# A pre-norm block with linear attention on one core: phase 1 without the V projection, wo scaled by rows

## The reference

```
y  = ln(x)
a  = ln(y) * ln1_g + ln1_b
q, k, v = a @ wq, a @ wk, a @ wv                     # 16 heads of 16
phi(t) = elu(t) + 1 = min(exp(t), 1) + relu(t)
kv = sum over tokens of phi(k)^T v,  z = sum of phi(k)   # per sequence and head
r  = y + ((phi(q) kv) / (phi(q) z + 1e-6)) @ wo
h  = ln(r) * ln2_g + ln2_b
s  = r + gelu(0.1 * clip(round(h @ w1 / 0.1))) @ w2       # w1 256x1024, w2 1024x256
x1 = x + s
out = x1 + (ln(x1) @ CB^T) * SCB / 127 + bias
```

## Time and profile before

| | |
|---|---|
| median of 3 runs | 613.63 us |
| profiled execution | 617.22 us, span 615.5 us |
| TensorE busy | 582.9 us (95%) |
| VectorE busy | 469.2 us (76%) |
| ScalarE busy | 411.4 us (67%) |
| GpSimd busy | 382.2 us (62%) |
| fp32 and fp32r products at L929, turns at L947 | 66% and 8% of the chain that ended last |
| HBM read, written | 20.45 MB, 8.39 MB |

### The profile page before, as it was taken

The page is one execution under the profiler, slowest core; times in us unless marked ns, Lnnn a source line. Parts: engine busy times, 40 slices in busy tenths (PEclk is TensorE's granted clock), DMA queues, the critical chain, the costliest instruction groups (busy, mean ns, idle before and its releaser), DMA issues.

```text
span 615.5 us, 12217 instructions
## 1 busy us (share of the span) xinstructions
PE 582.9 (95%) x3838; PEld 519.2 (84%) x3838; DVE 469.2 (76%) x1076; ACT 411.4 (67%) x767; POOL 382.2 (62%) x337
## 2 busy tenths in 40 slices
PE   6999999999998989999999999999999999999894
PEld 6887787778887879898999988989989899998784
DVE  5589888988777357878778787777787877878645
ACT  2277675767657658677687686866867768768660
POOL 3554647474443256777757768677677775776662
PEclk9599999999999799999999999999999999999998
DMA  8212120212110101101011011010110101100001
...
DMA packets 11128, 29.16 MB, mean 47 GB/s; under 512 B 2016, under 2 KB 4576, under 8 KB 11104
## 3 DMA queue, kind: packets, MB, share of 16 engines
...
HBM read 20.45 MB, written 8.39 MB: 47 GB/s over the span
## 4 chain that ended last, share of the span: by engine, by line
PE 74%; DVE 10%; issue 7%; ACT 4%; POOL 3%; DMA 1%; DVEq 0%; ACTq 0%; POOLq 0%; SPq 0%
PE psum L929 66%; PE psum L947 8%; DVE f_arena L673 2%; POOL f32r_arena L350 2%; DVE bn_stats L631 2%; DVE f_arena L658 1%; DVE scale_shift L648 1%; ACT f_arena L564 1%; ACT grid_index L553 1%; ACT f32r_arena L566 1%; DMA f_arena<-in_L_attn_x_dram 1%; ACT f_arena L486 1%; DVE w_lo L842 0%; DVE f_arena L908 0%; DVE mean_var L638 0%
## 5 line engine op out<-in xcount | busy, mean ns | idle before, releaser
L929 PE MATMUL psum<-w_hi,f32r_arena 128*128 128x256 f32 x1280 | 178.6, 286 | 4.3 <-POOL f32r_arena L350 3.2
L929 PEld LDWEIGHTS psum<-w_hi,f32r_arena 128*128 128x128 f32 x1280 | 165.8, 191 | 14.8 <-issue 7.9
L929 PE MATMUL psum<-f32r_arena,w_hi 128*128 128x512 f32 x512 | 142.0, 409 | 4.3 <-issue 3.7
L350 POOL TENSOR_TENSOR f32r_arena<-f_arena,f32r_arena 128x512 fp32r<-128x512 f32 x64 | 82.7, 1293 | 90.3 <-DVE f_arena L745 54.4
L553 ACT ACTIVATE grid_index<-psum,w_bias_in_steps 128x512 int8<-128x512 f32 x128 | 87.1, 680 | 75.4 <-PE psum L929 75.4
L929 PE MATMUL psum<-f32r_arena 128*128 128x512 f32 (+1 forms) x512 | 120.6, 378 | 2.6 <-issue 1.5
L929 PEld LDWEIGHTS psum<-f32r_arena,w_hi 128*128 128x128 f32 x512 | 89.8, 191 | 23.3 <-ACT grid_index L553 5.6
L929 PEld LDWEIGHTS psum<-f32r_arena 128*128 128x128 f32 x512 | 83.2, 190 | 14.9 <-issue 3.1
L564 ACT ACTIVATE f_arena<-grid_index 128x512 f32<-128x512 int8 x128 | 81.0, 633 | 18.7 <-POOL f32r_arena L350 10.4
L566 ACT ACTIVATE f32r_arena<-grid_index 128x512 fp32r<-128x512 int8 x128 | 79.3, 620 | 0.0
L947 PE MATMUL psum<-ident,f_arena 128*128 128x128 f32 x504 | 67.9, 279 | 4.8 <-DVE f_arena L658 3.4
...
## 6 DMA issues: line engine op xcount, KB each, us to landing
...
```

Of the source, the lines that this page charges most:

```text
L350: nc.gpsimd.tensor_tensor(t_lo[m % SLOTS], tf[m % 2], t_hi[m % SLOTS].bitcast(F32), ALU.subtract).then_inc(s["t_lo_p"], 1)
L929: return nc.tensor.matmul(out_, lhs, rhs, start=start, stop=stop, skip_group_check=True)
```

## The change

V isn't projected in phase 1. The gather sums phi(k)^T [n1, 1] instead, with n1 the normalised chunk as it stands (256 columns and ones, 257); n1 has two buffers for it. From the sums G of a sequence, VectorE makes G * gain + z * bias (key_sums), TensorE turns them (turn_sums), multiplies by wv in plain fp32 (blocks), and finalize cuts out the heads' blocks. For sequence 0 this lies in chunks 8 to 10, for sequence 1 in phase 2's first body. The key projection works on two tiles at once: one bank holds K of two tiles, exp and relu take 512 columns, relu stays in PSUM, VectorE's key feature reads it there. The low part of a chunk is made by VectorE, not GpSimd. The query's exp and relu of chunk c are done during chunk c+1, and its feature too. The weights for phase 2 are split in 4 slices of 1152 columns, in the first 8 chunks. The first steps of phase 2's chunk 0 stand in chunks 10 to 15, one in each, and the projection of w1's bias in chunk 8. The second half of phase 1 is written out without a loop.

Each row of wo is divided by its largest absolute value (VectorE makes scale and reciprocal, GpSimd the high part and the rest); the scale goes into the attention output where its high and low parts are written. The rest counts into flag 2, and where it is zero the third wo product is left out in chunks 1 to 15. The scratch for descriptors of GpSimd's DMAs is set to 1024.

```diff
-KVW = P + 1
+KVW = D + 1
+PT = TT // 2
...
-    SLICES = PAIRS - 2
+    SLICES = PAIRS // 2
...
+    def split_wo():
+        g.wait_ge(s["wo_inverse"], 1)
+        for k in range(KT):
+            nc.gpsimd.tensor_scalar(fm(wo_hi[:, :])[:, k], fm(wo_raw)[:, k], wo_inv[:, k:k + 1], 0.0, ALU.mult,
+                                    ALU.add).then_inc(s["wo_hi_done"], 1)
+        g.wait_ge(s["wo_hi_done"], KT)
+        for k in range(KT):
+            nc.gpsimd.tensor_scalar(fm(wo_rest[:, :])[:, k], fm(wo_hi[:, :])[:, k].bitcast(F32), wo_scale[:, k:k + 1], 0.0,
+                                    ALU.mult, ALU.add).then_inc(s["wo_parted"], 1)
+        g.wait_ge(s["wo_parted"], KT)
+        nc.gpsimd.tensor_tensor(wo_rest[:, :], wo_raw, wo_rest[:, :], ALU.subtract).then_inc(s["wo_left"], 1)
+        g.wait_ge(s["wo_left"], 1)
+        for k in range(KT):
+            nc.gpsimd.tensor_scalar(fm(wo_lo[:, :])[:, k], fm(wo_rest[:, :])[:, k], wo_inv[:, k:k + 1], 0.0, ALU.mult,
+                                    ALU.add).then_inc(s["wo_lo_done"], 1)
...
-            if within(c + 1):
-                low1(c + 1, 1 - p)
-            if within(c + 3):
-                power1(c + 3, 1 - p)
-            if is_chunk(c, CHUNKS - 3):
+            if within(c + 2):
+                power1(c + 2, p)
+            if is_chunk(c, PER_SEQ):
+                split_wo()
...
+    def k_pair(c, h):
+        n = c * 2 + h
+        pb = bank(PP + h)
+        a.wait_ge(s["k_pair"], n + 1)
+        a.wait_ge(s["phi_k_done"], n + 1)
+        act(e_k[h], pb, ACT.Exp)
+        act(pb, pb, ACT.Relu).then_inc(s["exp_k"], 1)
+    def q_exps(c):
         a.wait_ge(s["q_ready"], c + 2)
         wait(a, s["phi_q_ready"], c + 1)
         act(e_q, psum[:, QB:QB + KT, :].rearrange("p k n -> p (k n)"), ACT.Exp)
+    def q_relus(c):
         act(relu_q, psum[:, QB:QB + KT, :].rearrange("p k n -> p (k n)"), ACT.Relu).then_inc(s["q_exp"], 1)
...
+            act(fm(dst)[:, k], bank(b + k), ACT.Copy,
+                scale=wo_scale[:, k:k + 1] if done == "s_hi_a" else 1.0).then_inc(s[done], 1)
...
         for p in range(2):
             c = it * 2 + p
-            k_tile(c, 0)
+            if past(c, 1):
+                q_exps(c - 1)
+            k_pair(c, 0)
             if within(c + 1):
                 gain1(c + 1)
             if is_chunk(c, CHUNKS - 1):
                 high_h(0)
+            k_pair(c, 1)
+            if past(c, 1):
+                q_relus(c - 1)
...
-        wait(v, s["n1_turned"], c)
+        wait(v, s["kv_done"], c * 2)
...
+    def low1(c, p):
+        v.wait_ge(s["hi1"], c + 1)
+        ve.tensor_tensor(n_lo[p], a1, n_hi[p].bitcast(F32), ALU.subtract).then_inc(s["lo1"], 1)
+    def phi_key(c, h):
+        n = c * 2 + h
+        v.wait_ge(s["exp_k"], n + 1)
+        v.wait_ge(s["kv_done"], n + 1)
+        ve.scalar_tensor_tensor(out=phi_k[h], in0=e_k[h], scalar=1.0, in1=bank(PP + h),
                                 op0=ALU.min, op1=ALU.add).then_inc(s["phi_k_done"], 1)
...
+    def key_sums(seq):
+        v.wait_ge(s["kv_done"], 2 + (seq + 1) * PER_SEQ * 2)
...
+        for k in range(KT):
+            i = ve.tensor_tensor(g3[:, k], bank(KV + k)[:, 0:D], gb_rows[:, 0:D], ALU.mult)
+        i.then_inc(s["g_scaled"], 1)
...
+        v.wait_ge(s["g_scaled"], seq + 1)
+        for k in range(KT):
+            i = ve.scalar_tensor_tensor(out=g3[:, k], in0=gb_rows[:, D:2 * D], scalar=bank(KV + k)[:, D:KVW], in1=g3[:, k],
+                                        op0=ALU.mult, op1=ALU.add)
+        i.then_inc(s["g_sums"], 1)
...
+    def finalize(seq, b):
+        v.wait_ge(s["kv_tile2"], seq + 1)
+        src = bank(b)[:, 0:D].rearrange("p (k n) -> p k n", k=KT)
...
+        ve.tensor_tensor(blocks[:, :, 0:P], src, mask[:, :].unsqueeze(1).to_broadcast([P, KT, P]),
+                         ALU.mult).then_inc(s["kv_ready"], 1)
...
+            if done == "s_lo_a":
+                ve.scalar_tensor_tensor(out=fm(lo_)[:, k], in0=bank(b + k), scalar=wo_scale[:, k:k + 1],
+                                        in1=fm(hi_)[:, k].bitcast(F32), op0=ALU.mult,
+                                        op1=ALU.subtract).then_inc(s[done], 1)
...
+            if is_chunk(c, PER_SEQ + 2):
+                finalize(0, TP + 1)
+            if within(c + 2):
+                stats1(c + 2, p, it + 1)
             phi_key(c, 0)
...
             phi_key(c, 1)
+            if is_chunk(c, PER_SEQ + 1):
+                flag_value(PP, 2, "flag2")
+            if past(c, 1):
+                phi_query(c - 1)
+            if within(c + 1):
+                low1(c + 1, 1 - p)
+            if is_chunk(c, PER_SEQ):
+                v.wait_ge(s["wo_lo_done"], KT)
+                ve.tensor_reduce(flag_cols[:, 2 + SLICES:3 + SLICES], wo_lo[:, :].bitcast(F32), AX.X, ALU.max,
+                                 apply_absolute_value=True).then_inc(s["w_flag"], 1)
...
+            if is_chunk(c, PER_SEQ + 1):
+                turned_sums(0, TP)
+            if is_chunk(c, PER_SEQ + 2):
                 attend(0, 0)
+            if is_chunk(c, PER_SEQ + 3):
+                attend(0, 1)
+            if is_chunk(c, PER_SEQ + 4):
+                attn_low(0)
             if within(c + 2):
                 norm1(c + 2, p)
+            if is_chunk(c, PER_SEQ + 5):
                 first_residual(0)
+            if is_chunk(c, PER_SEQ + 6):
+                norm2(0)
...
     v.wait_ge(s["masks_made"], 3)
-    finalize(0)
+    key_sums(0)
+    v.wait_ge(loaded["wo"], 16)
+    for k in range(KT):
+        i = ve.tensor_reduce(wo_scale[:, k:k + 1], fm(wo_raw)[:, k], AX.X, ALU.max, apply_absolute_value=True)
+    i.then_inc(s["wo_max"], 1)
+    v.wait_ge(s["wo_max"], 1)
+    ve.tensor_scalar(wo_scale[:, :], wo_scale[:, :], 1e-30, None, ALU.max).then_inc(s["wo_scaled"], 1)
+    v.wait_ge(s["wo_scaled"], 1)
+    ve.reciprocal(wo_inv[:, :], wo_scale[:, :]).then_inc(s["wo_inverse"], 1)
+    for it in range(PER_SEQ // 2, PAIRS):
         pair(it)
+    low_h(0)
+    key_sums(1)
+    attend(1, 0)
+    attend(1, 1)
+    phi_query(CHUNKS - 1)
...
+        def key_pair(c, p, h):
+            n = c * 2 + h
+            if h == 0:
                 pe.wait_ge(s["hi1"], c + 1)
                 pe.wait_ge(s["lo1"], c + 1)
+            if is_chunk(n, 2 * (PER_SEQ + 2)):
+                pe.wait_ge(s["flag2"], 1)
+            pe.wait_ge(s["phi_k_done"], n + 1)
+            for r in range(2):
+                cols = slice((2 * h + r) * P, (2 * h + r + 1) * P)
+                terms = []
+                for k in range(KT):
+                    hi, lo = fm(n_hi[p])[:, k, cols], fm(n_lo[p])[:, k, cols]
+                    terms += [(hi, wkh[:, k]), (lo, wkh[:, k])]
+                    if not exact:
+                        terms.append((hi, wkl[:, k]))
+                i = products(bank(PP + h)[:, r * D:(r + 1) * D], terms, True)
+            i.then_inc(s["k_pair"], 1)
+        def gather(c, p, h):
+            n = c * 2 + h
+            first = h == 0 and (is_chunk(c, 0) or is_chunk(c, PER_SEQ))
+            if is_chunk(n, 2 * PER_SEQ):
+                pe.wait_ge(s["g_sums"], 1)
+            pe.wait_ge(s["phi_k_done"], n + 3)
+            for r in range(2):
+                for k in range(KT):
+                    i = mm(bank(KV + k)[:, 0:KVW], phi_k[h][:, r * D + k * P:r * D + (k + 1) * P],
+                           tm1(n1[p])[:, 2 * h + r], start=first and r == 0)
             i.then_inc(s["kv_done"], 1)
...
+        def pair(it):
             for p in range(2):
                 c = it * 2 + p
+                key_pair(c, p, 0)
                 if within(c + 1):
+                    turn1(c + 1, 1 - p)
+                if is_chunk(c, CHUNKS - 1):
+                    turn2(0)
+                key_pair(c, p, 1)
+                if is_chunk(c, PER_SEQ):
+                    pe.wait_ge(s["a1_ready"], c + 2)
+                    project_bias(TP)
+                gather(c, p, 0)
+                if is_chunk(c, PER_SEQ + 1):
+                    pe.wait_ge(s["a1_ready"], c + 2)
+                    turn_sums(0, TP)
+                    pe.wait_ge(s["flag_max"], 2)
+                    pe.wait_ge(s["phi_k_done"], 2 * c + 3)
+                    turn_flag(4 + SLICES, PP)
+                if is_chunk(c, PER_SEQ + 2):
                     pe.wait_ge(s["a1_ready"], c + 2)
                     pe.wait_ge(s["kv_ready"], 1)
                     attention(0, 0, 0)
+                if is_chunk(c, PER_SEQ + 3):
+                    pe.wait_ge(s["a1_ready"], c + 2)
+                    attention(0, 0, 1)
+                if is_chunk(c, PER_SEQ + 4):
                     pe.wait_ge(s["a1_ready"], c + 2)
                     turn_attention(0)
+                if is_chunk(c, PER_SEQ + 5):
                     pe.wait_ge(s["a1_ready"], c + 2)
+                    pe.wait_ge(s["wo_lo_done"], KT)
+                    attention_out(0, True)
+                gather(c, p, 1)
+                query(c, p)
```

(40 more changed lines are left out.)

345 lines of the change are left out of this document (135 added, 210 removed).

## The result

| | before | after |
|---|---|---|
| median of runs | 613.45 us (611.93 to 613.82, 4 runs) | 592.86 us (592.13 to 594.68, 4 runs) |
| profiled execution (span) | 617.22 us (615.5) | 594.68 us (592.9) |

What follows compares the result with a forecast made beforehand. TensorE was taken to bound phase 2, and a cycle of all engines phase 1. Phase 1 -19, boundary and first body +2.5, phase 2 -11.9 sum to -28.4 from 613.6: 585.2, rounded up to 585.5 us, range 574 to 603.

Steps and rivals of the forecast that it cites:

- TensorE's floor of 8.1: Phase-1 chunk: TensorE's own work falls from 9.5 to 8.1 us without the V projection, despite the wider gather.
- the loop of 9.0: Phase-1 chunk: hand-overs among TensorE, ScalarE and VectorE end the second gather at 9.0 us; chunk taken as 9.15.
- rival 4: The gap only shrinks in phase 1: chunks at 9.9 us, +11, 597 us; chance 0.12.
- rival 2: Phase 1: VectorE leaves GpSimd's power no opening; 11.1 us in chunks 1 to 7, 610 us in all; chance 0.08.
- the rule that I had weighed: Shared SBUF ports: two-input VectorE instructions keep out GpSimd's SBUF reads; moving the split frees key features, blocks the power more.
- Start at 18.8: Phase 1 starts at 18.8 us instead of 26.11, without the bias projection ahead of it; a gain of 7.3.
- Chunk 8, 5 us extra: Phase 1: key sums, row scales, bias projection and the wo split add 5 us to chunk 8, from 3 to 10.
- The sum to the boundary: Start and chunks of phase 1 sum to 178 us plus 0.4 of tail, against 197.5: -19.
- First body, +2.5: Phase 2's first body gains attention, turns and fp32 products and a later low part: +2.5 us, from 1 to 5.
- Phase 2, -11.9: Phase 2: dropping the third wo product saves 0.97 less 0.12 us in 14 bodies: -11.9, from 0 to -14.6.
- rival 1: Third product's saving hidden in phase 2, as VectorE's and GpSimd's chains don't follow: 597 us; chance 0.09.
- rival 3: wo's rests aren't zero, so all of phase 2 takes its general branch: 733 us; chance 0.05.

Runs made afterwards that it cites:

- experiment 6: Kernel after with eight unused TensorE matmuls ahead of the first gather in chunks 0 to 7 of phase 1; 600.28 us.
- experiment 7: Kernel after with VectorE's largest value of a w_lo slice taken over 8 columns, not 768, in odd chunks 1 to 7; 594.05 us.
- Experiment 8: Kernel after with second keys ahead of the gain on ScalarE and their key feature ahead of the cast on VectorE; 602.52 us.
- Experiment 9: Kernel after with phase 1's low part moved from VectorE back to GpSimd, behind the power; 600.61 us.
- experiment 11: Kernel after with the flag of wo taken in chunk 9 instead of chunk 8; 591.67 us.
- Experiment 12: Kernel after with the edits of experiment 4 and experiment 11, and phase 1's last query feature between the halves of chunk 1's attention; 584.29 us.
- experiment 2: Kernel before with the third wo product left out in phase 2, without the scale by row; 602.56 us.
- experiment 4: Kernel after with the MLP's last low part on VectorE and GpSimd's final add waiting for it; 586.51 us.

## Why the prediction was right, and where it was off

- **TensorE's floor of 8.1 and the loop of 9.0 in a phase-1 chunk: right.** The floor is 8.08 (experiment 6), the chunk 9.19 for 9.15, so rival 4 (9.9) didn't happen. TensorE doesn't set it (experiment 6), nor does a full VectorE (experiment 7). That the loop of hand-overs does is what remains, and what TensorE's waits for the key features (L703) say; no run made the loop shorter and the chunk with it. Experiment 8, meant for that, shows what the working lacked: a second path, through gain, cast, low part and normalising, sets the chunk at 9.74 once the gain stands behind the second keys.
- **The power starves (rival 2): did not happen.** Before, 5.21 was the one long case of 16, the others took 1.64 to 2.82. After, it took 1.64 to 2.83 in chunks 1 to 7, and VectorE never waited for it there. Experiment 9 shows the other half of the rule that I had weighed: the split on GpSimd blocks VectorE, some 0.5 us a chunk.
- **Start at 18.8: 17.73.** VectorE's first shift took 1.25 for 2.30.
- **Chunk 8, 5 us extra: 6.8.** The bias products took 5.44 for 3.5 and ran with the gathers behind them at mean clocks of 0.66 and 0.67; I had priced them at the full clock, though a fall of the clock behind an idle TensorE was among my reasons for the range. That VectorE's wait is behind it was priced at 2 and is worth 1.4 (experiment 11). The sum to the boundary came out by luck: phase 1 ended at 180.44 for 178.4, 2.0 late, but the 3.73 us of branch, which I had left as they were, shrank to 0.96, and phase 2 began at 181.40 for 182.1. Its first products then ran at a clock of 1.00, not 0.50 as before.
- **First body, +2.5: +4.65**, and nearer +7 at equal clock. The place was named (VectorE's first low part late), its followers weren't: the attention's rest, 2.37, and the low part behind the sums' copy and the residual, 1.78. Experiment 12 took most of the first wait away (1.42 to 0.28); what holds the other two wasn't tried.
- **Phase 2, -11.9: -7.4.** This step failed, and it is rival 1 in part. I took the whole 0.97 less 0.12 because everything behind the projection starts from its end. GpSimd's chain doesn't: its add of 2.40 us now ends after the statistics (320.33 to 322.73) and holds the power (322.82), and from there low parts, ScalarE's gelu and the normalisation reach the last low part 0.46 us too late. Of 0.97, 0.54 was seen; 0.24 is hidden without any scale (experiment 2); moving the last low part off GpSimd brings a body to 24.05, the whole 0.97 (experiment 4).
- **Rests not zero (rival 3)**: did not happen: no w_lo product ran in phase 2 and no third wo product beyond chunk 0.

The profiled execution of before lay 3.6 us above its median, that of after 1.8, which takes another 2 us off the difference of the medians.
